# Two transformer layers on one core: norms, routers and projections of one batch as side tasks of the other batch's stages, and a mixture with one bank each for gate and up

## The reference

```
x = LN(x + causal attention with 16 heads of width 128)
x = LN(x + mixture 0: softmax over 8 experts, best 2 rescaled, silu(gate)*up, plus a shared part of 704 with a sigmoid gate)
x = LN(x + grouped attention: 16 heads of width 16, 4 key groups, biases)
x = LN(x + mixture 1: softmax plus bias over 16 experts, best 6, silu(gate)*up with biases, plus a shared part of 352)
```

## Time and profile before

| what | us |
|---|---|
| time, median of 3 runs (lowest, highest) | 2349.77 (2338.06, 2356.79) |
| the profiled execution's own time | 2343.43 |
| its span | 2341.7 |
| PE, DVE, ACT, POOL busy in the span | 2163.5, 1502.5, 1206.6, 556.0 |
| mean granted clock of PE | 0.949 |

### The profile page before, as it was taken

How to read it: one execution, slowest core, us unless ns; L and a number is a source line. 1 busy time by engine, 2 the same in 40 slices (tenths; PEclk the granted TensorE clock), 3 DMA queues, 4 the chain that set the end, 5 groups by cost and what they waited for, 6 DMA issues and landing times. The chain is left out here.

```text
span 2341.7 us, 31637 instructions
## 1 busy us (share of the span) xinstructions
PE 2163.5 (92%) x11008; PEld 1626.0 (69%) x11008; DVE 1502.5 (64%) x2543; ACT 1206.6 (52%) x2421; POOL 556.0 (24%) x539
## 2 busy tenths in 40 slices
PE   7999999999999999769999859999998589999996
PEld 5888888888888888648878633333334368878885
DVE  4666666666666666636656647888881546646665
ACT  4656555556555555434434323777775334433442
POOL 2434343434343333202222100000000012222220
PEclk9999999999999999969999965999999689999998
DMA  2000000000000000001111020000000011111111
GB/s 77 15 24 14 23 15 23 15 17 20 14 24 8 24 13 10 3 26 49 50 45 47 16 49 11 17 22 19 18 15 5 1 46 52 49 41 41 52 49 45
DMA packets 54220, 64.55 MB, mean 28 GB/s; under 512 B 9115, under 2 KB 34502, under 8 KB 54086
## 3 DMA queue, kind: packets, MB, share of 16 engines
q1 hardware_dynamic: 54086, 62.81, 9.7%
HBM read 52.68 MB, written 2.10 MB: 23 GB/s over the span
## 5 line engine op out<-in xcount | busy, mean ns | idle before, releaser
L1356 POOL TENSOR_TENSOR a_pr<-a_pr,a_rinv 128x128 f32<-128x128 f32 (+7 forms) x256 | 293.9, 1148 | 505.6 <-DVE a_rinv L1578 505.6
L1042 DVE TENSOR_REDUCE a1m_negm<-psum 128x1 f32<-128x1024 f32 x256 | 301.5, 1219 | 54.5 <-PE psum L920 53.8
L1023 ACT ACTIVATE a1m_pt<-psum 128x512 f32<-128x512 f32 x512 | 268.3, 602 | 86.9 <-PE psum L935 86.6
L647 DVE SCALAR_TENSOR_TENSOR f_hid<-psum,f_bias_now,f_act_s 128x512 f32<-128x512 f32 x168 | 126.0, 750 | 269.7 <-ACT f_act_s L604 199.3
L604 ACT ACTIVATE f_act_s<-psum,f_bias_now 128x512 f32<-128x512 f32 x168 | 115.8, 689 | 337.2 <-PE psum L71 263.7
L504 POOL TENSOR_TENSOR f_lo_gu<-f_raw_gu,f_hi_gu 128x512 fp32r<-128x512 f32 x84 | 109.0, 1297 | 741.5 <-ACT f_hi_gu L579 741.5
L69 PE MATMUL psum<-xh,f_hi_gu 128*128 128x512 f32 x672 | 265.8, 396 | 1.8 <-POOL f_lo_gu L504 1.1
L71 PE MATMUL psum<-xh,f_lo_gu 128*128 128x512 f32 x672 | 264.2, 393 | 0.0
L70 PE MATMUL psum<-xl,f_hi_gu 128*128 128x512 f32 x672 | 263.8, 392 | 0.0
L1499 ACT ACTIVATE a_pth<-psum 128x512 fp32r<-128x512 f32 (+3 forms) x384 | 174.7, 490 | 142.0 <-PE psum L1411 139.5
L1492 ACT ACTIVATE a_pr<-psum,a_negm 128x128 f32<-128x128 f32 (+7 forms) x256 | 190.3, 743 | 72.3 <-DVE a_negm L1569 66.6
(11 more groups left out here) (226 smaller groups left out, 4899.6 us busy)
## 6 DMA issues: line engine op xcount, KB each, us to landing
f_raw_gu<-in_gu SPq DMA_DIRECT2D x84, 256.0 KB, 2.7
f_raw_dn<-in_down SPq DMA_DIRECT2D x84, 128.0 KB, 2.0
a_wr<-in_qkv SPq DMA_DIRECT2D x32, 256.0 KB, 2.8
a_wvr<-in_qkv SPq DMA_DIRECT2D x32, 128.0 KB, 2.6
a_wor<-in_o SPq DMA_DIRECT2D x32, 128.0 KB, 2.1
a_qq<-a_qhi SPq DMA_DIRECT2D x128, 32.0 KB, 1.9
yT<-in_xT SPq DMA_DIRECT2D x4, 512.0 KB, 6.6
a_qq<-a_qlo SPq DMA_DIRECT2D x64, 32.0 KB, 1.9
```

What stands on the lines that cost most here:

```text
L1023: act.activation(pt[:, s % SLOTS, g, :], st_ps[:, n % 3, :], ACT.Exp, scale=1.0 / HD1).then_inc(exp_done, 1)
L1042: dve.tensor_reduce(negm[:, u % 2, g * NQ + q:g * NQ + q + 1], mx_ps[:, bank, :, :], AX.XY, ALU.max, negate=True).then_inc(mx_taken, 1)
L1356: pool.tensor_tensor(pr[j][:, 0:n], pr[j][:, 0:n], rinv[:, j:j + 1].to_broadcast([P, n]), ALU.mult).then_inc(p_done, 1)
```

## The change

The stages after the first attention are cut by batch. Norm, router, projections of keys, queries and values, and output projection become classes (`NormHalf`, `RouterHalf`, `QKVHalf`, `OutHalf`) whose work is a list of small tasks, each of one bank: PE fills it, ACT rounds, DVE empties. A `Ring` counts these uses for all stages. Tasks are hosted by other stages:

- The first attention, from head 1 of batch 1 on, hosts norm and router of batch 0, one task in some query tiles, on its two task banks.
- Mixture 0 begins with the spreading of batch 0's router weights, hosts in its first half norm and router of batch 1, and in its second half the second norm and the projections of batch 0.
- `in_turn` blocks on eight banks do what has no host: norm and projections of batch 1 (p1); output, norm and router of batch 0 (p2); the last norm of batch 1 (p3).
- Mixture 1 hosts output, norm and router of batch 1, then the last norm of batch 0, whose store it also issues.

The mixture is written out without loops. Gate and up have one bank each, y four, and two are left for side tasks. The order on PE per 512 tokens is gate, up, down of the tile before, and one side task if planned. The halves follow each other without a pause: y of the second half begins a tile late, per 512 tokens, when ACT has copied that part out. Silu and product take their biases straight from the table. A norm half takes all its roots in one task (`root`), on its 8 token tiles; statistics and rounding go through `yT` in place. In the first attention the probabilities are stored without their masked blocks, by another numbering of the same tiles. The grouped attention itself is the same but for separate tensors by batch.

The core of the new code (unchanged helpers and the classes' like methods left out):

```diff
+class Ring:
+    def __init__(self, counters, banks):
+        self.banks, self.counters = banks, counters
+        self.filled, self.rounded, self.emptied = counters.filled, counters.rounded, counters.emptied
+        self.at, self.hi = {}, {}
+    def add(self, key, rounds):
+        self.at[key] = len(self.at)
+        self.counters.uses += 1
+        if rounds:
+            self.hi[key] = len(self.hi)
+            self.counters.roundings += 1
+    def bank(self, key):
+        return self.banks[self.at[key] % len(self.banks)]
+    def room(self, key):
+        n = self.at[key] - len(self.banks) + 1
+        return self.use0 + n if n > 0 else 0
+    def count(self, key):
+        return self.use0 + self.at[key] + 1
+    def hi_count(self, key):
+        return self.rounding0 + self.hi[key] + 1
+def free_bank(pe, ring, key):
+    if ring.room(key) > 0:
+        pe.wait_ge(ring.emptied, ring.room(key))
+    return ring.bank(key)
...
+    def tensor(self, pe, t, ring):
+        kind, key = t[0], (self.name, t)
+        if kind == "root":
+            return
+        o = free_bank(pe, ring, key)
+        t0 = self.tokens(t[1]).start
+        if kind == "nf":
+            for sem, n in self.ready(t[1], ring):
+                pe.wait_ge(sem, n)
+            for q in range(2):
+                for dt in range(DT):
+                    i = pe.transpose(o[:, q * D + dt * P:q * D + (dt + 1) * P],
+                                     self.yT[:, dt, t0 + q * P:t0 + (q + 1) * P], self.ident[:])
+        else:
+            pe.wait_ge(self.xn_done, self.nth * self.TILES + 2 * t[1] + 2)
+            for q in range(2):
+                for dt in range(DT):
+                    i = pe.transpose(o[:, dt * 2 * P + q * P:dt * 2 * P + (q + 1) * P],
+                                     self.yT[:, q, t0 + dt * P:t0 + (dt + 1) * P], self.ident[:])
+        i.then_inc(ring.filled, 1)
...
+    def vector(self, dve, t, ring):
+        kind, key = t[0], (self.name, t)
+        if kind == "root":
+            dve.wait_ge(self.std_done, self.nth + 1)
+            dve.reciprocal(self.rstd[:], self.std[:]).then_inc(self.rstd_done, 1)
+            dve.wait_ge(self.rstd_done, self.nth + 1)
+            for n in range(self.TILES):
+                x = self.yT[:, n % 2, self.tokens(n // 2)]
+                dve.tensor_scalar(x, x, self.mv[:, n, 0:1], self.rstd[:, n:n + 1],
+                                  ALU.subtract, ALU.mult).then_inc(self.xn_done, 1)
+            return
+        dve.wait_ge(ring.rounded, ring.hi_count(key))
+        o = ring.bank(key)
+        if kind == "nf":
+            n = 2 * t[1]
+            dve.bn_stats(self.stats[:, n, :], o[:, 0:D])
+            dve.bn_stats(self.stats[:, n + 1, :], o[:, D:2 * D]).then_inc(ring.emptied, 1)
+            dve.wait_ge(ring.emptied, ring.count(key))
+            for q in range(2):
+                dve.bn_aggr(self.mv[:, n + q, :], self.stats[:, n + q, :]).then_inc(self.mv_done, 1)
+            return
+        x = self.tokens(t[1])
+        dve.tensor_tensor(self.xl[:, :, x], o.rearrange("p (a n) -> p a n", a=2), self.xh[:, :, x].bitcast(F32),
+                          ALU.subtract).then_inc(ring.emptied, 1)
...
+    SIDE = [(norm, t) for t in FORE] + [(norm, ("root",))] + [(norm, t) for t in BACK] + [(router, t) for t in CHOOSE]
+    SPOTS = [(hb, qt) for hb in range(H0 + 1, H0 + 8) if hb % VG for qt in (1, 2, 4, 5, 7)]
...
+            def gate(K, c):
+                if c == 0:
+                    pe.wait_ge(lo_gu_done, K + 1)
+                if K * NC + c >= 1:
+                    pe.wait_ge(silu_done, K * NC + c)
+                for dt in range(DT):
+                    w0 = dt * P
+                    i = mm3(pe, gate_ps, hi_gu[:, K % 2, w0:w0 + P], lo_gu[:, K % 2, w0:w0 + P],
+                            xh[:, dt, tokens(K, c)], xl[:, dt, tokens(K, c)], dt == 0, dt == DT - 1)
+                i.then_inc(gate_done, 1)
+            def up(K, c):
+                if K * NC + c >= 1:
+                    pe.wait_ge(prod_done, K * NC + c)
+                for dt in range(DT):
+                    w0 = (DT + dt) * P
+                    i = mm3(pe, up_ps, hi_gu[:, K % 2, w0:w0 + P], lo_gu[:, K % 2, w0:w0 + P],
+                            xh[:, dt, tokens(K, c)], xl[:, dt, tokens(K, c)], dt == 0, dt == DT - 1)
+                i.then_inc(up_done, 1)
...
+            for side, t in fore:
+                side.tensor(pe, t, ring)
+            for K in range(2 * NT + 1):
+                for c in range(NC):
+                    if K <= LAST:
+                        gate(K, c)
+                        up(K, c)
+                    if K >= 1:
+                        if (K - 1) % NT == 0:
+                            begin_y(K - 1, c)
+                        down(K - 1, c)
+                    for side, t in plan.get((K, c), ()):
+                        side.tensor(pe, t, ring)
...
+            for K in range(2 * NT + 1):
+                if K <= LAST:
+                    silu(K, 0)
+                if K >= 1:
+                    keep_hi(K - 1, 1)
+                    for side, t in plan.get((K - 1, 1), ()):
+                        side.scalar(act, t, ring)
+                if K < LAST:
+                    round_gu(K + 1)
+                if K <= LAST:
+                    keep_hi(K, 0)
+                if K >= 1 and K % NT == 0:
+                    keep_y(K - 1, 0)
+                if K <= LAST:
+                    silu(K, 1)
+                    round_dn(K)
+                for side, t in plan.get((K, 0), ()):
+                    side.scalar(act, t, ring)
+                if K >= 1 and K % NT == 0:
+                    keep_y(K - 1, 1)
+                if K == 1:
+                    for o in begins:
+                        if isinstance(o, (Projection, RouterWeights)):
+                            o.scalar(act)
...
+            for K in range(2 * NT + 1):
+                if K >= 1:
+                    keep_lo(K - 1, 1)
+                if K <= LAST:
+                    product(K, 0)
+                if K >= 1:
+                    for side, t in plan.get((K - 1, 1), ()):
+                        side.vector(dve, t, ring)
+                if K <= LAST:
+                    keep_lo(K, 0)
+                for side, t in plan.get((K, 0), ()):
+                    side.vector(dve, t, ring)
+                if K <= LAST:
+                    product(K, 1)
+                if K == 1:
...
+    def sync(self, sp, ring):
+        sp.wait_ge(self.cleared, 1)
+        sp.wait_ge(ring.emptied, ring.count((self.name, ("pj", 2, 1))))
+        for r in range(2):
+            for x, src in enumerate((self.khi, self.klo, self.khi)):
+                for g in range(2):
+                    p0, d0 = r * HALFP + x * HD1, (r * 2 + g) * HD1
+                    sp.dma_start(self.ks[p0:p0 + HD1, g, :].bitcast(F32), src[d0:d0 + HD1, :].bitcast(F32)).then_inc(self.k_in, 16)
+        sp.wait_ge(self.k_in, 16 * 12)
...
+        def norm_slots(o, back=True):
+            slots = tasks(o, FORE) + PAUSE + [(o, ("root",))]
+            return slots + PAUSE * 2 + tasks(o, BACK) if back else slots
+        def router_slots(r):
+            return tasks(r, CHOOSE[:2]) + PAUSE + tasks(r, CHOOSE[2:3]) + PAUSE + tasks(r, CHOOSE[3:]) + PAUSE + maps(r)
+        def place(first, slots):
+            return {(first + n // 2, n % 2): [side] for n, side in enumerate(slots) if side is not None}
...
+            causal_attention(nc, "a0", counters, a, xh, xl, yT, ident, idr, eps, psum, rw0, n0a, r0a)
+                    plan = {**place(0, norm_slots(n0b) + PAUSE + router_slots(r0b)),
+                            **place(NT0 + 1, norm_slots(n1a) + PAUSE + tasks(x0, PROJECT))}
+                    mixture(nc, "f0", counters, w0, xh, xl, yT, idr, psum, True, (r0a, r0b), maps(r0a), plan, n1a, (wqkv, x0))
+                    in_turn(nc, "p1", counters, psum, tasks(n1b, FORE + [("root",)] + BACK) + tasks(x1, PROJECT), (x1, wo, rw1))
+                grouped_attention(nc, "a1", qhi, qlo, ks, vs, z, ident, psum)
+                in_turn(nc, "p2", counters, psum, tasks(o1a, TURN + GATHER) + tasks(n2a, FORE + [("root",)] + BACK) + tasks(r1a, CHOOSE))
+                plan = {**place(0, tasks(o1b, TURN) + PAUSE + tasks(o1b, GATHER) + PAUSE + norm_slots(n2b) + PAUSE +
+                                router_slots(r1b)),
+                        **place(NT1 + 1, norm_slots(n3a, False))}
+                mixture(nc, "f1", counters, w1, xh, xl, yT, idr, psum, False, (r1a, r1b), maps(r1a), plan, n3a, (), (n3a, rows, stored, 0))
+            in_turn(nc, "p3", counters, psum, tasks(n3b, FORE + [("root",)]), (), (n3b, rows, stored, NormHalf.GROUPS))
```

More of the change, by code:

```diff
@@ L1171, in causal_attention, with enlist @@
+FORE = [("nf", s) for s in range(4)]
+BACK = [("nb", s) for s in range(4)]
+CHOOSE = [("lg", 0), ("lg", 1), ("lt",), ("ex",), ("pick",), ("weigh",)]
+def enlist(ring, tasks):
+    for side, t in tasks:
+        if side.has_bank(t):
```

(12 more changed lines are left out.)

1852 lines of the change are left out of this document (917 added, 935 removed).

## The result

The changed kernel took 2259.58 us (median of 4 runs, 2251.94 to 2265.86), the kernel before 2352.5 beside it; the ratio is 0.9621, 95% interval 0.9584 to 0.9658. The profiled execution spans 2262.2 us, 79.5 less than before.

What follows compares the result with a forecast made beforehand. PE, busy for 92% of the span, fills the mixtures; 272.2 us between stages wait on hand-overs. Terms sum to −74.8 us against 2343.43, giving 2269 us; forecast's own range 2252 to 2290, overall 2236 to 2320.

Steps and rivals of the forecast that it cites:

- Hosting costs its matmuls: Both mixtures: hosted tasks cost PE 23.2 and 21.4 us of side work, plus stalls; the mixtures grow 26.2 and 26.4.
- Stalls: PE waits in the mixtures behind hosted roots (1.0 to 1.3 us each) and choosing (3.5): 7.5 and 7.6 us.
- One bank is enough: Mixture loops: with one bank each for gate and up, slack of 0.9 us keeps the loop at PE's pace.
- Plain tiles stay as they were: Mixtures: tiles without side work keep 8.3 us (34 tiles, first) and 8.16 us (50 tiles, second).
- Attention to mixture: Stretch from first attention to first mixture: 62.1 us shrinks to 10.3, −51.8; could be 7 or 14.
- Standing halves: Half stages before second attention, before second mixture and at the end: 40.9, 51.2 and 17.9 us (−25.6, −52.3, −8.0).
- Rival 2: Half stages are chains and do not halve, taking 85% of their present length: +56, 2325 us; chance 0.07.
- Second attention: Unchanged at 390.8 us: 0, with 13 us either way for the low clock at its start.
- First attention: Hosting norm and choosing of batch 0 adds 7.3 us on PE and 3 us of bursts: +10.3.
- rivals, 5: Side tasks wait for their producer at the head of PE's queue, so as much stands: 2335 to 2350; chance 0.05.
- 6: Rival: more than forecast, by a warm second attention start (−13) or no stalls (−15): 2240 to 2252; chance 0.12.
- a rule of the Trainium skill: ScalarE's table loads: a drain of about 1.38 us each makes ACT's added time in full stages 37 us, not 18.

Runs made afterwards that it cites:

- written out: The kernel before with the tiles of both mixtures written out instead of run in hardware loops of two: 2336.78 us, ratio 0.9987.
- both last versions: Changed kernel with queries fetched ahead, first bias table last and mixture buffers moved: second's 10 KB up (2247.92 us), or both at 128 modulo 256 bytes (2249.03 us).
- last version: Changed kernel with both mixtures' buffers at 128 modulo 256 bytes, bias table last, and one unit's queries fetched ahead: 2249.03 us, ratio 0.9577.
- standing: Changed kernel with nothing hosted in the two mixtures, their tasks in blocks between the stages: 2305.21 us, ratio 0.982; with two banks each for gate and up 2311.91 us.
- moved: The kernel before with an unused buffer of 22,656 bytes a partition ahead of the mixtures' working buffers: 2356.96 us, ratio 1.002.
- bias table last: Changed kernel with each mixture's bias table allocated behind the other buffers instead of second: 2261.64 us, ratio 0.9648.
- early queries: Changed kernel with two units' queries fetched ahead, the second mixture's buffers 10 KB up and the first's bias table last: 2247.92 us, ratio 0.9561.
- old order: Kernel with nothing hosted and two banks each for gate and up, TensorE's order put back to gate, up, gate, up, down, down: 2304.78 us, ratio 0.9832.

## Why the forecast held

1. *Hosting costs its matmuls.* Right, and the term on which all hung: 23.2 and 21.4 us of side work, 7.5 and 7.6 of stalls, against 27.0 and 25.2 measured for both together; on PE the work took 24.9 and 23.2. *Stalls* were too large: they stand against PE's idle 3.7 and 3.1. A root was taken as 1.0 to 1.3 and was 0.6; choosing was taken as 3.5 and was 1.27 and 1.08.
2. *One bank is enough.* Right (1 us between one and two).
3. *Plain tiles stay as they were.* This step failed. I took 8.3 and 8.16 us from the earlier trace rows as what PE needs; 8.37 and 8.33 came, 2.4 and 8.5 us more over 34 and 50 tiles. In the second mixture that outweighs the 4.5 us by which the stalls were overrated. (The two figures are upper ones: the better place gave back 6.7 of the 8.5.) The runs put in its place: the rewriting moved the buffers, and with them the pitch of every matmul.
4. *Attention to mixture*, −52.7 for −51.8: right in its parts too, maps at the low clock included.
5. *Standing halves*: 35.4, 44.2 and 12.7 for 40.9, 51.2 and 17.9, each 5 to 7 us too long. Mis-sized in all three was the root with its table, taken as 5.6 us in a chain; from the root to the last subtraction it is 3.3 us, because the load runs while VectorE still aggregates and because subtracting in place takes 0.33 us a tile (2.67 for eight), not the 0.475 of the earlier trace rows. That explains 2.3 us of each. Of the rest, 1.4 us are the statistics (first and last: the root starts 6.6 us into the stretch, not 8.0), 1.5 turning back and projecting (first), 4.3 the router (second: 8.7 us from the last turned half to the weights, not 13.0) and 1.4 the exit with the store (last). The queries' 8.9 us behind the block were right. Rival 2 is refuted.
6. *Second attention.* 0 was right for the change; the +5.8 is a start 4.9 us shorter and a tail 10.8 longer, both seen with either code. The forecast allowed for the start alone.
7. *First attention.* Right, +11.6 for +10.3; PE's added work is 9.4 us and not 7.3.

The pitch and the second attention cost 17 us more than forecast, stalls and standing halves 26 less, the rest (side work on PE 3.5, first attention 1.3) nearly 5 more: −4.7 in all, against the execution's own time. That the sum came so near is in part luck: errors of 21 and 26 us cancel, and 10.8 of the 21 are a tail that other executions of the same code don't have. Against the medians 2269 was 9 us too high. Of the rivals, 5 is refuted by the table above (9.4 + 35.4 + 44.2 us stand where 62.1 + 66.5 + 103.5 did) and 6 came true for half of the stalls alone.

On tables I had weighed a rule of the Trainium skill (ScalarE: Activation LUTs, What ACT_TABLE_LOAD costs) that adds a drain of about 1.38 us to a load. The rows show none that PE or ScalarE loses here: the rounding ends at 1028.48, the load starts at 1028.50, the root 0.01 us after the load's end. By that rule the eight hosted loads would have held ScalarE an estimated 21 us, by the rows 10; taking them away gave PE back 2.

## What to carry to other kernels

A stage whose main engine is full can still host a chain of small work: it pays for the matmuls and about 0.1 us a task (more than half of it behind the few tasks with a long chain), here half of what the chain costs standing alone, provided each slot's answer fits the slack of the loop.
|---|---|---|
| 128 | 8.16 | before and written out, second mixture; both last versions, second; last version, first |
| 64 | 8.28 | before, first |
| 0 | 8.32 to 8.34 | changed, standing and moved, second; bias table last and early queries, first |
| 192 | 8.34 | moved, first |
| 32 | 8.38 | bias table last, second |
| 160 | 8.37 (8.35 in the old order) | changed and standing, first |

Fastest is the place that `xh` and `xl` have. Whether the period is 256 bytes or 512 is open, since all four fast places are alike modulo 512 too. Which pair of buffers meets, and through which port, no run isolates. The slow pitch seems to need the other engines at work: at the very end of the changed kernel's second mixture, when they are nearly done, ten matmuls take 2.27 us, 0.227 each (timeline, PE):

```profile
2246.83 0.39 PE L70 MATMUL psum<-f_hl,f_hi_dn 128*128 128x512 f32 x1
...
2249.10 0.39 PE L71 MATMUL psum<-f_hh,f_lo_dn 128*128 128x512 f32 x1
```

The Trainium skill (TensorE: Matmul & The Clock Gate, Back-to-back issue gap) gives 512 columns about 216 ns at the full clock for a matmul by itself, and about 131 ns in a stream of weight loads and matmuls. In the streams here the best place has 227 and the worst 233, so the second figure doesn't hold for them, and neither knows of a place.

The granted clock can stay at 1.2 GHz for long while PE is busy. In the changed kernel PE was busy for 39.2 of the 44.8 us between the first maxima at 1351.0 and the rise:

```profile
1341.20:1395.80 54.60, 39.18 (x96) 16.25 (x96) 37.35 (x32) 9.65 (x17) 0.00 (x0) 0.50 0.10 22
```

This fall came in an idle wait. Those in 5 of 13 tails did not: PE had been busy for 8.2 to 8.9 of the 10 us before, and the low level lasted 27 to 34 us, to the end of the tail. What decides on the tails stays open.
